# Another order in the router's second loop, in the first squares and variances of the last pass, and in its last tile

## What is computed

```python
x = _layernorm(x + attention(x))
base_out = einsum('btd,od->bto', x, base_W) + base_b        # 4096 x 4096
probs = softmax(einsum('btd,nd->btn', x, router_W) + router_b)   # 15 columns
w = top-8 of probs, added up per mapped expert                # 8 weights
h = einsum('btd,erd->bter', x, A)                             # 8 experts, rank 16
lora = einsum('bter,eor->bto', h * w, B) * 2.0
x = _layernorm(x + base_out + lora)
```

## Time and profile before

| what | value |
|---|---|
| median of 3 runs (lowest, highest) | 1345.12 us (1340.43, 1345.6) |
| the profiled execution's own time | 1340.14 us |
| its span, slowest core (core 7) | 1338.6 us |
| spans of all cores | 1306.2 to 1338.6 us |
| PE busy | 1219.9 us (91% of the span) |
| DVE busy | 779.6 us (58%) |
| ACT busy | 548.0 us (41%) |
| mean granted TensorE clock of core 7 | 0.958 |

### The profile page before, as it was taken

How to read it: one execution, slowest core, us unless ns; L and a number is a source line. 1 busy time by engine, 2 the same in 40 slices (tenths; PEclk the granted TensorE clock), 3 DMA queues, 4 the chain that set the end, 5 groups by cost and what they waited for, 6 DMA issues and landing times.

```text
span 1338.6 us, 29179 instructions; the slowest of 8 cores (1306.2 to 1338.6 us)
## 1 busy us (share of the span) xinstructions
PE 1219.9 (91%) x10768; PEld 962.4 (72%) x10768; DVE 779.6 (58%) x1502; ACT 548.0 (41%) x856; POOL 159.4 (12%) x323
## 2 busy tenths in 40 slices
PE   2199699999999999679989999999999899799995
PEld 1188588888888858557757667677788898577773
DVE  2230035778846935308867778787888752355654
ACT  0011011111111125567868778687711112477776
POOL 4000011101111112311211211111110000000000
PEclk9599899999999999889989989999999899999998
DMA  9899999999999989964595756655447025578876
GB/s 126 89 159 161 173 173 168 158 170 166 172 165 170 174 130 132 131 114 69 74 135 84 126 76 107 109 87 101 79 86 132 10 56 132 146 241 267 265 249 252
DMA packets 96860, 187.86 MB, mean 140 GB/s; under 512 B 15824, under 2 KB 46800, under 8 KB 94416
## 3 DMA queue, kind: packets, MB, share of 16 engines
q0 software_dynamic: 44160, 122.82, 60.8%
q1 hardware_dynamic: 52560, 63.17, 16.0%
...
## 4 chain that ended last, share of the span: by engine, by line
PE 75%; DMA 14%; ACT 3%; DVE 3%; issue 3%; another core or an unknown queue 1%; POOL 0%; ACTq 0%; DVEq 0%; SPq 0%; POOLq 0%
PE pF L522 61%; DMA xw<-xr 5%; DMA xs<-xr 4%; DMA w<-wt 4%; PE pS L601 3%; PE pN L622 2%; DVE xT L1044 2%; PE pS L660 1%; PE pS L555 1%; PE pS L563 1%; PE pS L574 1%; PE pN L574 1%; ACT p L739 1%; PE pS L561 1%
## 5 line engine op out<-in xcount | busy, mean ns | idle before, releaser
L522 PE MATMUL pF<-w,xT 128*128 128x256 bf16 x8192 | 950.3, 277 | 64.7 <-DMA w<-wt 54.1
L522 PEld LDWEIGHTS pF<-w,xT 128*128 128x128 bf16 x8192 | 800.8, 99 | 201.6 <-issue 98.7
L739 ACT ACTIVATE p<-pS 128x1024 bf16<-128x1024 f32 x256 | 248.1, 1021 | 75.5 <-PE pS L601 75.3
L708 ACT ACTIVATE zo<-pF 128x256 bf16<-128x256 f32 x224 | 86.1, 384 | 463.0 <-PE pF L522 463.0
L893 DVE TENSOR_REDUCE wqk<-wqs 128x64 bf16<-128x2048 bf16 x64 | 144.2, 2280 | 178.0 <-DMA wqs<-wq 177.9
L857 DVE TENSOR_REDUCE wr<-w 128x64 bf16<-128x2048 bf16 x52 | 189.6, 3656 | 17.9 <-DMA w<-wt 17.4
L1009 DVE SCALAR_TENSOR_TENSOR xr<-xr,ob 128x1024 bf16<-128x1024 bf16 x64 | 76.3, 1222 | 15.7 <-DMA xr<-xr 15.1
L814 ACT ACTIVATE jk<-zu 128x2048 bf16<-128x2048 bf16 x32 | 61.1, 1910 | 39.1 <-DVE zu L1124 25.7
L601 PE MATMUL pS<-qx,kx 32*128 32x512 bf16 x512 | 53.6, 392 | 24.8 <-ACT p L739 18.9
L322 POOL DMA_DIRECT2D w<-wt x64 | 34.0, 546 | 303.5 <-PE pF L522 183.9
L1114 DVE SCALAR_TENSOR_TENSOR zu<-brow,std,pF 128x256 bf16<-128x256 bf16 x32 | 15.3, 481 | 85.5 <-PE pF L538 85.5
...
## 6 DMA issues: line engine op xcount, KB each, us to landing
...
```

Source lines behind the costliest of these rows:

```text
L522: ins = te.matmul(pF[k % 2][:, 0:HW], xT[:, t, c, :], W[h % 2][:, c, :], start=(i == 0), stop=(close and i == NCH - 1))
L708: s_ge.inc(sc.activation(m[f"zo{k % n}"], pF[k % 2][:, 0:HW], AF.Copy))
L739: s_ex.inc(sc.activation(m[f"p{Q % 2 * 2 + half}"], pS[half], AF.Exp, scale=SCALE_Q))
```

## The change

Four edits; the matmuls and their operands stay the same.

1. **Router's second loop**, on TensorE and ScalarE: the unit (13, t - 6) goes ahead of `router(t)` (ScalarE: its `evict_z` ahead of `router_exp(t)`), where it stood behind `turn_h(t - 1)`. At the loop's end the unit (13, 10) goes ahead of `turn_h(15)`.
2. **First squares**, on ScalarE: the first half of tile 1's squares goes ahead of the second half of tile 0's; the second half of tile 1's stays where it was, behind tile 0's output.
3. **First variances**, on VectorE: u(14, 2) goes ahead of n(1), and the corrections c(2) ahead of y(1), so that y(1) and r(2) follow c(2).
4. **Last tile**: c(15) goes ahead of the units (14, 15) and (15, 15), on TensorE and on VectorE; on VectorE it also goes ahead of n(14) and y(14). The squares of tile 15 are three instructions, of columns 0 to 2048, 2048 to 3584 and 3584 to 4096, the first two of which need no unit of h = 14 or 15; the variance has one more instruction. The output's third quarter goes from ScalarE to VectorE, so each writes two, and SyncE stores them in the order 2, 0, 3, 1.

```diff
-for _t in range(2, T):
+for _t in range(2, T - 1):
     LASTPASS += [("u", 14, _t), ("u", 15, _t), ("c", _t)]
+LASTPASS += [("c", T - 1), ("u", 14, T - 1), ("u", 15, T - 1)]
...
-              ("u", 15, 1), ("r", 1), ("n", 0), ("y", 0), ("n", 1)]
-for _t in range(2, T):
-    LASTPASS_V += [("u", 14, _t)] + [("n", _t - 1)] * (_t > 2)
-    LASTPASS_V += [("u", 15, _t), ("y", _t - 1), ("c", _t), ("r", _t)]
-LASTPASS_V += [("n", T - 1), ("y", T - 1)]
...
+              ("u", 15, 1), ("r", 1), ("n", 0), ("y", 0),
+              ("u", 14, 2), ("n", 1), ("u", 15, 2), ("c", 2), ("y", 1), ("r", 2)]
+for _t in range(3, T - 1):
+    LASTPASS_V += [("u", 14, _t), ("n", _t - 1), ("u", 15, _t), ("y", _t - 1), ("c", _t),
+                   ("r", _t)]
+LASTPASS_V += [("c", T - 1), ("n", T - 2), ("u", 14, T - 1), ("y", T - 2), ("u", 15, T - 1),
+               ("r", T - 1), ("n", T - 1), ("y", T - 1)]
...
+SQ_COLS = {t: [(0, 2048), (2048, 4096)] for t in range(T - 1)}
+SQ_COLS[T - 1] = [(0, 2048), (2048, 3584), (3584, 4096)]
+SQ_ORDER = [(0, 0), (1, 0), (0, 1), (1, 1)]
...
                 for t in range(T):
-                    for q in range(4):
+                    for q in range(4) if t < T - 1 else (2, 0, 3, 1):
                         store_y(t, q)
...
                 for t in range(T - LAGR, T):
+                    plain(UIDX[(13, t - T + LAGR)])
                     router(t)
                     turn_h(t - 1)
-                    plain(UIDX[(13, t - T + LAGR)])
+                plain(UIDX[(13, LAGR)])
                 turn_h(T - 1)
-                for k in range(UIDX[(13, LAGR)], NEV):
+                for k in range(UIDX[(13, LAGR)] + 1, NEV):
                     plain(k)
...
                 for t in range(T - LAGR, T):
+                    evict_z(UIDX[(13, t - T + LAGR)])
                     router_exp(t)
                     copy_h(t - 1)
-                    if t > T - LAGR:
-                        evict_z(UIDX[(13, t - T + LAGR - 1)])
+                evict_z(UIDX[(13, LAGR)])
                 copy_h(T - 1)
...
-                    square_z(t, 0)
-                    square_z(t, 1)
+                    for i in range(len(SQ_COLS[t])):
+                        if (t, i) == (0, 1):
+                            square_z(1, 0)
+                        if (t, i) != (1, 0):
+                            square_z(t, i)
                     sc.wait_ge(s_ng.h, t + 1)
...
-                    for q in range(3):
+                    for q in range(3 if t < T - 1 else 2):
...
+                    for q in (3,) if t < T - 1 else (2, 3):
+                        if prior[t][q] is not None:
+                            r_y.landed(v, prior[t][q])
+                        s_yv.inc(v.tensor_scalar(
+                            out=yp[t][q], in0=m[f"zu{t % 2}"][:, q * 1024:q * 1024 + 1024],
+                            scalar1=m["rv2"], scalar2=m["nm2"], op0=ALU.mult, op1=ALU.add))
```

More of the change, by code:

```diff
@@ L218, in build_program @@
         place(regR, ("zu0", D, BF16), ("zu1", D, BF16), ("brow", D, BF16), ("jk", 2048, BF16),
-              *[(f"dg{i}", 128, BF16) for i in range(4)], ("su0", 9, F32), ("su1", 9, F32), ("sq20", 2, F32), ("sq21", 2, F32),
+              *[(f"dg{i}", 128, BF16) for i in range(4)], ("su0", 9, F32), ("su1", 9, F32), ("sq20", 3, F32), ("sq21", 3, F32),
               ("fcols", 10, F32))
@@ L473, in store_y @@
                 def store_y(t, q):
-                    if q < 3:
+                    if t == T - 1 and q == 2:
+                        sy.wait_ge(s_yv.h, T)
+                    elif t == T - 1 and q == 3:
+                        sy.wait_ge(s_yv.h, T + 1)
+                    elif q < 3:
                         sy.wait_ge(s_y.h, 3 * t + q + 1)
@@ L788, in _ @@
                 for t in range(T - LAGR, T):
+                    evict_z(UIDX[(13, t - T + LAGR)])
                     router_exp(t)
                     copy_h(t - 1)
-                    if t > T - LAGR:
-                        evict_z(UIDX[(13, t - T + LAGR - 1)])
+                evict_z(UIDX[(13, LAGR)])
                 copy_h(T - 1)
-                for k in range(UIDX[(13, LAGR - 1)], NEV):
+                for k in range(UIDX[(13, LAGR)] + 1, NEV):
                     evict_z(k)
@@ L802, in deviations, with square_z @@
                                            scale=m["std"][:, t:t + 1]))
-                def square_z(t, half):
-                    n = 2 * t + half
-                    sc.wait_ge(s_cu.h, NPAIR * t + (4 if half == 0 else NPAIR))
-                    if half == 1:
+                def square_z(t, i):
+                    first, end = SQ_COLS[t][i]
+                    n = SQ_NUM[(t, i)]
+                    sc.wait_ge(s_cu.h, NPAIR * t + (4 if i == 0 else NPAIR))
+                    if end == D:
                         sc.wait_ge(s_gd.h, UIDX[(15, t)] - NEV + 1)
@@ L814, in square_z @@
                     s_sq2.inc(sc.activation(
-                        m["jk"], m[f"zu{t % 2}"][:, 2048 * half:2048 * half + 2048], AF.Square,
-                        accum_out=m[f"sq2{t % 2}"][:, half:half + 1]))
+                        m["jk"][:, 0:end - first], m[f"zu{t % 2}"][:, first:end], AF.Square,
+                        accum_out=m[f"sq2{t % 2}"][:, i:i + 1]))
                 sc.wait_ge(s_std.h, 2)
@@ L1145, in row_var @@
                     own()
-                    put(v.scalar_tensor_tensor(m["e1"], sq[:, 1:2], 1.0 / D, m["e1"], ALU.mult,
-                                               ALU.add))
-                    own()
+                    for i in range(1, len(SQ_COLS[t])):
+                        put(v.scalar_tensor_tensor(m["e1"], sq[:, i:i + 1], 1.0 / D, m["e1"],
+                                                   ALU.mult, ALU.add))
+                        own()
                     s_ng.inc(v.scalar_tensor_tensor(m[f"nv{t % 2}"], m[f"ng{t % 2}"],
@@ L1154, in last_quarter @@
                     v.wait_ge(s_n2.h, t + 1)
-                    if prior[t][3] is not None:
-                        r_y.landed(v, prior[t][3])
-                    s_yv.inc(v.tensor_scalar(out=yp[t][3], in0=m[f"zu{t % 2}"][:, 3072:4096],
-                                             scalar1=m["rv2"], scalar2=m["nm2"], op0=ALU.mult,
-                                             op1=ALU.add))
+                    for q in (3,) if t < T - 1 else (2, 3):
[4 more added lines that the diff above has]
+                            scalar1=m["rv2"], scalar2=m["nm2"], op0=ALU.mult, op1=ALU.add))
                 for t in range(T):
```

4 lines of the change are left out of this document (3 added, 1 removed).

## The result

| | before | after |
|---|---|---|
| median (lowest to highest), 5 runs each, same chip | 1345.12 us (1340.43 to 1350.16) | 1333.56 us (1332.12 to 1338.08) |
| profiled execution, own time | 1340.14 us | 1333.52 us |
| span of the slowest core | 1338.6 us (core 7) | 1332.0 us (core 3) |

The ratio of the two kernels' times is 0.9937, with an interval of 0.9912 to 0.9962: faster, by 8.5 us of 1345 (5 to 12). (The two medians alone are 11.6 us apart, which lies inside that interval.) The prediction was 1335.7 us, range 1330 to 1342.

What follows compares the result with a forecast made beforehand. PE was taken to bound the kernel (91% busy, 75% of the chain). Core 0 slowest: 1337.6 - 3.5 - 7.8 + 2.9 = 1329.2, plus 1.5 makes 1330.7, 9.4 less; from the median 1345.12, 1335.7 us, range 1330 to 1342.

Steps and rivals of the forecast that it cites:

- The pauses: PE, router's loop and last pass: waits of 3.38 and 7.03 us and the slow units behind them go.
- Core 0's router term: Router's second loop on core 0: a gain of 1.8 + 1.7 = 3.5 us.
- late enough to find hb(7) ready: Router's loop, core 0: PE reaches turn_h(7) at 1063.3, when hb(7) is ready, so no new wait there.
- First tiles: Start of the last pass: PE's long pause in tile 2 goes, gaining 8.1 us on core 7, 7.8 on core 0.
- residual pauses: PE's seventh corrections in the last pass: waits of 0.2 us left in tile 2 and 1.4 in tile 3.
- Last tile: End of the last pass: n(14) starts 3.9 us later behind c(15), which waits for z; a loss of 2.9 us.
- (a): Rival: the last tile costs nothing or gains; time 1331 to 1333 us; chance 0.12.
- (b): Rival: the last pass's pause returns in tile 3, 5 us; first tiles gain 3 to 4; time 1341; chance 0.19.
- (c): Rival: the short new pauses cost clock, two slow units of 2.2 to 2.8 us each; time about 1341; chance 0.13.
- (d): Rival: slower, since loads of z land late, 14 us for 5.0 to 7.7; time 1352 and more; chance 0.06.
- The sum: Whole span: router, first and last tile terms add up to 1328.2 us on core 7, 1329.2 on core 0.
- a sign of being wrong: Whole kernel: a core other than 0 or 7 setting the time would show the forecast wrong.

Runs made afterwards that it cites:

- e8_split: The change, but on VectorE c(15) is divided: its first two pairs, then n(14), then the other five; ratio to before 0.9914.
- e10_order: e8_split, but with tile 15's squares, output and store order as before the change; ratio to before 0.9918.
- e5: The kernel before, with only the first half of tile 1's squares moved ahead on ScalarE; ratio to before 0.9985.
- e6: The kernel before, with only VectorE's new order, u(14, 2) ahead of n(1) and c(2) ahead of y(1); ratio to before 0.9956.
- e4_nolast: The change without its edit of the last tile; ratio to before 0.9934.
- e7_n14: The change, but with n(14) ahead of c(15) on VectorE; ratio to before 0.9911.

## Why the prediction was right, and where it was off

**The pauses.** Right in place and kind: no pause at `turn_h(5)`, 0.93 to 0.95 us at `turn_h(7)` on all cores (said 1.0), no pause over 1.01 us in the last pass (said 0.2 in tile 2 and 1.4 in tile 3), no slow unit in either stretch. The new pause of 1.4 us in tile 3 was not there on cores 7 and 0, for which it was worked out; four other cores have one of 0.37 to 0.93. I said -5.2 us for core 7's router loop: it went from 87.62 to 82.39.

**Core 0's router term was too large**: 3.5 said, 84.91 - 82.43 = 2.5 measured. The step that failed is that PE would come "late enough to find hb(7) ready". The 12.4 us from hb(5) to hb(7) hold: `turn_h(5)` and `turn_h(7)` stand 12.42 us apart on core 0 after, with a pause of 0.94 like on the other cores. What doesn't hold is PE's lateness. In the trace of before, core 0 came to the second loop 1.6 us later against VectorE than core 7 did (its pause at `turn_h(5)` is 1.81 us, core 7's 3.38), behind a pause at `turn_h(0)` with a slow unit; timeline of PE, core 0:

```profile
1020.94 0.27 PE L668 MATMUL pN<-idm,hb 128*128 128x128 bf16 x1 [3.42 <-DVE hb L1103]
1021.07 6.47 PE L522 MATMUL pF<-w,xT 128*128 128x256 bf16 x32
```

I took that for a property of the core, and it is an event of one execution: in the trace of after no core has a slow unit there. In all thirteen traces four cores of 104 have one (cores 0 and 1 of before, core 2 of e8_split, core 4 of e10_order), and they are the only four without the usual pause at `turn_h(5)` or `turn_h(7)`. Where the event comes with the new order, in e8_split and e10_order, the term comes out about as forecast: no pause at `turn_h(7)`, and a router stretch of 81.1 us (84.9 - 3.5 = 81.4 said). Timeline of PE, e8_split, core 2, `turn_h(0)` and `turn_h(7)`:

```profile
1009.56 0.27 PE L681 MATMUL pN<-idm,hb 128*128 128x128 bf16 x1 [3.51 <-DVE hb L1121]
1009.68 6.44 PE L535 MATMUL pF<-w,xT 128*128 128x256 bf16 x32
...
1051.77 0.22 PE L681 MATMUL pN<-idm,hb 128*128 128x128 bf16 x1
```

**First tiles**: 8.1 and 7.8 said for cores 7 and 0, 59.99 - 50.42 = 9.6 and 59.69 - 50.39 = 9.3 measured. The mechanism holds (e5, e6); the gain was put too low by the residual pauses, 1.6 together by my working, none on these two cores and 0.7 on the mean of eight. z(2, 3) was late as said on core 3 (landed 8.1 us after its issue, 7.7 said), but n(2) and y(2) stacked up less behind it: they wait 0.86 and 0.81 us there.

**Last tile**: +2.9 said, +3.5 on the mean, +2.8 on core 0 and +4.7 on core 7. Counted from tile 14's row sum (at 1338.6 - 24.21 = 1314.39 on core 7 before, at 1332.0 - 28.12 = 1303.88 on core 3 after), by the prediction's own steps:

| step | before | after | difference | said |
|---|---|---|---|---|
| n(14) starts | 2.70 | 7.87 | 5.2 | 3.9 |
| tile 14's output on ScalarE | 5.04 | 9.86 | 4.8 | 3.7 |
| squares of tile 15 | 9.76 | 13.27 | 3.5 | 2.4 |
| tile 15's output | 16.08 | 20.29 | 4.2 | 3.3 |
| end | 24.21 | 28.12 | 3.9 | 2.9 |

The first step carries the whole miss: the last piece of z landed 8.29 us after its issue, not 6.5 (issued 0.4 us earlier against the row sum, it landed 1.4 later). Why it took 1.8 us longer no run settles. From the squares on the terms hold. The three squares take 1317.15 to 1321.74, 4.6 us, where two take 4.15 (tile 14's, on the same core): the third costs 0.44, taken as 0.6. The last stores give back 0.3 us (8.13 to 7.83 from the output's start to the end), taken as 0.4.

The Trainium skill ("ScalarE: Activation LUTs", the section on table loads) gave 186 ns plus 0.833 ns per column. That is 1.47 and 0.61 us for 1536 and 512 columns. This trace agrees, with 1.48 and 0.63. The third square's 0.44 us is more than the 0.2 worked out from the page, because each square also brings a read of the accumulator and a gap. Timeline of ACT, core 3, the read behind the second square:

```profile
1320.67 0.19 ACT L829 ACTIVATION_READ_ACCUMULATOR jk<-zu 128x1 f32 x1
```

The Trainium skill ("DMA: Bandwidth & Descriptors", the section on the anatomy of one DMA) gives for GpSimd's path a rule by which each 512 KB store would land 3.2 us after its issue, and the last tile lose 1.0. These stores are issued by SyncE, and the trace disagrees with the figure; the tile view of y, core 3, for the last four stores:

```profile
DMA to landing us min/median/max: 2.7/4.0/4.8
```

The quickest is under the page's figure and the slowest half as long again: for these four, issued within 1.8 us, no one price per store holds.

**Rivals.** (a) named 1331 to 1333 us, about where the time came out, but for a last tile that costs nothing; the last stretch is 3.5 us longer, so the time came from the other two terms and (a) fell. (b), the pause coming back in tile 3, did not happen in this trace: at most 0.93 us. It does happen on single cores: the same orders show 3.17 us there on core 4 of e4_nolast and 3.66 on core 2 of e10_order, whose first tiles then take 56.0 us. Cores 1, 5 and 6 of e7_n14, with the same orders up to there, have 2.17 to 2.75 us in tile 2 or 3 and a slow unit, and take 54.3 to 54.7. It is rarer and smaller than (b) had it, but the trace of after was one without it. (c) fell for the pauses of this change's trace, though e6 and e7 show it for pauses twice as long. (d), late landings, hardly happened in the first tiles (on core 3, z(2, 0) took 5.7 us where 5.0 was taken, z(2, 3) 8.1 where 7.7), and 1.8 us of it did in the last.

**The sum** came out partly by luck. On core 7 it said -5.2 - 8.1 + 2.9 = -10.4, and -5.2 - 9.6 + 4.7 = -10.1 was measured: the first tiles' term was 1.5 too small, the last tile's 1.8 too small, and they cancel. On core 0 it said -8.4, and -2.5 - 9.3 + 2.8 = -9.0 was measured, again with two errors of opposite sign. The mean core has -8.4. And the core that set the time was neither 7 nor 0, which the prediction had named as a sign of being wrong. Core 3 gained 86.14 - 82.45 = 3.7 and 59.09 - 51.93 = 7.2 us and lost 28.11 - 24.21 = 3.9, so 7.0. It ends at 1332.0 because it was late before the stretches began: it came to `turn_h(4)` at 1047.0, core 7 at 1019.7, where in the trace of before they came at 1029.2 and 1044.3. Nothing in the prediction could name the slowest core of the next execution; what it could name is the amount per core, and that it had about right.
